# One DMA queue for all maxima, and the queries' staging buffer moved, in the second attention of a one-core kernel

## The reference

```python
B, T, _ = resid.shape                     # 2, 512, 512; 32 heads of 16, 8 key heads, groups of 4
q = (resid @ Wq).reshape(B, T, N_HEADS, D_HEAD).transpose(0, 2, 1, 3)
k = (resid @ Wk).reshape(B, T, N_KV_HEADS, D_HEAD).transpose(0, 2, 1, 3)
v = (resid @ Wv).reshape(B, T, N_KV_HEADS, D_HEAD).transpose(0, 2, 1, 3)
q = q * cos + _rotate_half(q) * sin
k = k * cos + _rotate_half(k) * sin
att = einsum('bhgqd,bhkd->bhgqk', q.reshape(B, 8, 4, T, 16), k) / sqrt(16)
att = where(causal, att, -inf)
ctx = einsum('bhgqk,bhkd->bhgqd', softmax(att), v)
out = ctx.reshape(B, 32, T, 16).transpose(0, 2, 1, 3).reshape(B, T, 512) @ Wo
```

## Time and profile before

| | |
|---|---|
| median of three runs | 950.86 us |
| profiled execution: its own time | 948.68 us |
| profiled execution: span from first to last instruction | 946.9 us |
| PE busy | 912.7 us (96%) |
| DVE busy | 772.8 us (82%) |
| ACT busy | 598.5 us (63%) |
| POOL busy | 617.5 us (65%) |
| attention B from the first exponential | 761.2 us on |
| granted TensorE clock, mean over the span | 0.998 |

### The profile page before, as it was taken

One profiled execution on the slowest core, in us unless ns is written; L12 is line 12 of the kernel. 1 busy time (PEld: TensorE's weight loads), 2 busy tenths in 40 slices (PEclk: granted clock), 3 DMA queues, 4 the chain that ended last, 5 costly groups with the idle time before them and its releaser, 6 DMA issues.

```text
span 946.9 us, 19835 instructions
## 1 busy us (share of the span) xinstructions
PE 912.7 (96%) x6720; PEld 488.5 (52%) x6720; DVE 772.8 (82%) x1812; ACT 598.5 (63%) x1323; POOL 617.5 (65%) x668
## 2 busy tenths in 40 slices
PE   5899999999999999999999999999999989999998
PEld 2455555555555555545555555554545534444553
DVE  6878887887888888687788888888988889996864
ACT  4677666676666666666666666656464469997331
POOL 4788876968768687696877868722459755553211
PEclk9999999999999999999999999999999999999999
DMA  9176386483665637647366564764342943121145
GB/s 338 43 192 173 70 203 136 75 209 87 130 181 107 145 81 192 145 70 205 78 147 176 101 145 96 135 165 86 69 88 53 177 87 58 42 43 24 24 90 156
DMA packets 256005, 114.10 MB, mean 120 GB/s; under 512 B 244144, under 2 KB 244784, under 8 KB 251312
## 3 DMA queue, kind: packets, MB, share of 16 engines
q1 hardware_dynamic: 246400, 70.41, 39.9%
q10 hardware_dynamic: 9520, 42.50, 13.1%
HBM read 49.84 MB, written 2.10 MB: 55 GB/s over the span
## 4 chain that ended last, share of the span: by engine, by line
PE 76%; DVE 11%; ACT 6%; DMA 4%; issue 2%; POOL 1%; SPq 0%; ACTq 0%; DVEq 0%; POOLq 0%
PE bank L1258 15%; PE bank L1259 15%; PE bank L1260 15%; PE bank L1739 4%; PE bank L1357 3%; PE bank L1359 3%; PE bank L1358 3%; PE bank L1377 3%; PE bank L1379 3%; PE bank L1378 3%; PE bank L1671 2%; PE bank L1645 2%; DMA bw_lo<-bw_hi 2%; ACT bank L988 1%; DVE bank L1969 1%
## 5 line engine op out<-in xcount | busy, mean ns | idle before, releaser
L621 POOL TENSOR_TENSOR rt<-rt 128x512 f32<-128x512 f32 x80 | 101.4, 1272 | 133.1 <-DVE rt L1954 133.1
L1986 DVE SCALAR_TENSOR_TENSOR bw_hi<-bank,rden,bw_hi 128x128 f16<-128x128 f32 (+3 forms) x256 | 123.3, 544 | 61.0 <-ACT bw_hi L1024 61.0
L988 ACT ACTIVATE bank<-bank,shift,c_score 128x128 f32<-128x128 f32 (+3 forms) x256 | 147.3, 605 | 2.1
L1969 DVE CUSTOM_DVE_ANT_0 bank<-bank,mask_w 128x512 f32<-128x512 f32 (+3 forms) x256 | 117.9, 521 | 21.5 <-PE bank L1359 21.5
L1024 ACT ACTIVATE bw_hi<-bank,rden 128x128 f16<-128x128 f32 (+3 forms) x256 | 114.5, 535 | 22.7 <-DVE rden L1979 22.7
L983 ACT ACTIVATE shift<-smax,c_score 128x4 f32<-128x4 f32 x64 | 19.0, 297 | 155.5 <-DVE smax L1969 155.5
L628 POOL TENSOR_TENSOR arena<-rt,arena 128x512 f16<-128x512 f32 x80 | 92.3, 1157 | 8.8 <-ACT arena L972 7.9
L1259 PE MATMUL bank<-xt,wq_hi 128*128 128x512 f16 x256 | 97.0, 379 | 0.4 <-issue 0.3
L1258 PE MATMUL bank<-wo_hi,arena 128*128 128x512 f16 x256 | 97.0, 379 | 0.0
L1259 PE MATMUL bank<-wo_lo,arena 128*128 128x512 f16 x256 | 97.0, 379 | 0.0
L1260 PE MATMUL bank<-wo_hi,arena 128*128 128x512 f16 x256 | 97.0, 379 | 0.0
(11 more groups left out here) (241 smaller groups left out, 2455.2 us busy)
## 6 DMA issues: line engine op xcount, KB each, us to landing
qcode<-in_q_codes ACTq DMA_DIRECT2D x7, 1024.0 KB, 4.9
qscale<-in_q_scales ACTq DMA_DIRECT2D x7, 1024.0 KB, 7.2
ocode<-in_o_codes ACTq DMA_DIRECT2D x7, 1024.0 KB, 4.9
oscale<-in_o_scales ACTq DMA_DIRECT2D x7, 1024.0 KB, 7.7
kvcode<-in_k_codes ACTq DMA_DIRECT2D x8, 256.0 KB, 7.5
kvcode<-in_v_codes ACTq DMA_DIRECT2D x8, 256.0 KB, 7.8
kvscale<-in_k_scales ACTq DMA_DIRECT2D x8, 256.0 KB, 8.0
kvscale<-in_v_scales ACTq DMA_DIRECT2D x8, 256.0 KB, 9.6
```

The source lines that it names most:

```text
L988: act.activation(a_rows(i, s), a_rows(i, s), ACT.Exp, bias=shift[:, s % 2, c:c + 1], scale=c_score[:, 0:1], accum_out=bank[3][:, SUMS_AT + ...
L1969: dve.tensor_tensor_reduce(bank[bk][:, o:o + (i + 1) * P], bank[bk][:, o:o + (i + 1) * P], mask_w[:, S - (i + 1) * P:S], 1.0, LOWEST, ALU. ...
L1986: dve.scalar_tensor_tensor(out=p_row[:, s % 2, LO_AT[i]:LO_AT[i] + P_STEP * i + 1:P_STEP], in0=turned_back(i, s), scalar=rden[:, s % 2, c: ...
```

## The change

It has four parts. (1) `q_stack` becomes a view of the second half of `ctx_b`, and with that ScalarE's wait in set 1 goes. (2) ScalarE's two placings are taken off its stream: SyncE issues all of them. (3) `turn_queries` of tiles 6 and 7 leave the place between the first turns of maxima and go to SyncE's rounds 4 and 6; `turn_keys` of tiles 6 and 7, in rounds 3 and 4 before, are in rounds 3 and 5. (4) From set 2 on each placing of pair 0 stands directly behind its own turn, ahead of the turn of pair 1. The separate semaphores of sets 0 and 1 are folded into `d_mturn`.

```diff
-        q_stack = staged("q_stack", [P, 2, B_HEADS * B_ST], F16)
         stage.close()
+        q_stack = ctx_b[:, ST:NT].rearrange("p t n -> p (t n)").bitcast(F16).rearrange("p (i n) -> p i n", i=2)
...
             sp.wait_ge(stacks_set, 2)
             for t in range(NT - 2):
                 turn_queries(t)
                 turn_keys(t)
-            turn_max(0, 0)
-            place_max(sp, 0, 0)
-            turn_max(0, 1)
-            turn_queries(NT - 2)
+            for c in range(2):
+                turn_max(0, c)
+                place_max(0, c)
             turn_max(1, 0)
-            place_max(sp, 1, 0)
             turn_max(1, 1)
-            turn_queries(NT - 1)
+            place_max(1, 0)
+            place_max(1, 1)
             for q in range(2, SETS):
                 turn_max(q, 0)
-                if 3 <= q < 5:
-                    turn_keys(NT - 5 + q)
+                place_max(q, 0)
                 turn_max(q, 1)
-                place_max(sp, q, 0)
-                place_max(sp, q, 1)
+                if q in (3, 5):
+                    turn_keys(NT - 2 + (q - 3) // 2)
+                elif q in (4, 6):
+                    turn_queries(NT - 2 + (q - 4) // 2)
+                place_max(q, 1)
...
-                    if q == 1 and i == 5:
-                        act.wait_ge(d_q[0], 16 * HALF)
-                        act.wait_ge(d_q[1], 16 * HALF)
...
-                if q == 0:
-                    b_exps(q, range(2))
-                    place_max(act, q, 1)
-                    b_exps(q, range(2, LOADS - 2))
-                elif q < SETS:
+                if q < SETS:
                     b_exps(q, range(LOADS - 2))
                 if 1 <= q <= SETS:
                     b_ctx_out(q - 1)
                 if q < SETS:
                     b_exps(q, range(LOADS - 2, LOADS))
-                if q == 0:
-                    place_max(act, 1, 1)
```

More of the change, by code:

```diff
@@ L363, in build @@
         rk1, rk2 = (hs[:, 1, c0:c0 + 2 * P].rearrange("p (i n) -> p i n", i=2) for c0 in (0, 2 * P))
-        staged("before_q_stack", [P, 2, KV_HEADS * 2 * B_ST], F16)
-        q_stack = staged("q_stack", [P, 2, B_HEADS * B_ST], F16)
         stage.close()
+        q_stack = ctx_b[:, ST:NT].rearrange("p t n -> p (t n)").bitcast(F16).rearrange("p (i n) -> p i n", i=2)
         pt = sb("pt", [P, 8, TRI], F32)
@@ L428, in build @@
         d_mturn = [sem(f"d_mturn{c}") for c in range(2)]
-        d_mfirst = [[sem(f"d_mfirst{c}{i}") for i in range(2)] for c in range(2)]
         d_m = [sem(f"d_m{i}") for i in range(3)]
@@ L460, in m_place @@
             return n % 3, 16 * (n // 3 + 1)
[L462 to L473, removed]
         def rows_landed(c, t):
@@ L543, in turn_max, with place_max @@
                 sp.dma_start_transpose(m_turned[:, q % 2, c].rearrange("p (i n) -> p i n", n=P),
-                                       m_stack[:, q % 2, c].rearrange("p i n -> p (i n)")).then_inc(max_turned(q, c)[0], 16)
+                                       m_stack[:, q % 2, c].rearrange("p i n -> p (i n)")).then_inc(d_mturn[c], 16)
+            def place_max(q, c):
+                j, b = set_place(q)
+                sp.wait_ge(d_mturn[c], 16 * (q + 1))
+                for f in range(2):
+                    two = slice(f * P // 2 + MAX_AT, f * P // 2 + MAX_AT + 2)
+                    sp.dma_start(qt_b[two, 2 * j + c, b * S:(b + 1) * S], m_turned[two, q % 2, c]
+                                 ).then_inc(d_mrows[c][q % 2], 16)
             sp.wait_ge(stacks_set, 2)
@@ L802, in _ @@
             twice = float(np.full(2, MAX_W, np.float16).view(np.float32)[0])
-            pool.memset(q_stack[:].rearrange("p i n -> p (i n)").bitcast(F32).rearrange(
+            pool.memset(q_stack.rearrange("p i n -> p (i n)").bitcast(F32).rearrange(
                 "p (g w) -> p g w", w=B_ST // 2)[:, :, MAX_AT // 2:], 0.0).then_inc(stacks_set, 1)
@@ L839, in b_split @@
                 if q >= 2:
-                    pool.wait_ge(*max_turned(q - 2, c))
+                    pool.wait_ge(d_mturn[c], 16 * (q - 1))
                 pool.tensor_tensor(low, m, max_dn[:].unsqueeze(1).broadcast_to([P, ST, 2]), ALU.mult).then_inc(bsplit, 1)
```

## The result

The changed kernel took 964.84 us (median of four runs, 963.87 to 968.37), the kernel before 950.75 on the same terms. The ratio is 1.0161 with a 95% interval of 1.0147 to 1.0176: 15.3 us slower by the ratio (14.1 us lie between the two medians). The profiled execution took 965.24 us at a span of 963.5; before it was 948.68 at 946.9, so 16.6 us lie between the two traces.

| stretch | before | after | difference |
|---|---|---|---|
| span's start to the first exponential | 761.15 | 761.87 | +0.7 |
| to the start of set 2 | 18.22 | 15.75 | -2.5 |
| set 2 to the start of set 6 | 27.06 | 38.06 | +11.0 |
| set 6 to the start of set 15 | 62.84 | 70.50 | +7.7 |
| set 15 and the blocks behind it | 77.6 | 77.3 | -0.3 |

A forecast was written before the change was run, and what follows sets the result against it. PE, ACT and DVE nearly fill attention B's steady part; after the change SyncE's rounds would bind. 5.3 us at set 8, entry gain included, plus 6.0 behind it gave +11.3: 962 on the median, range 954 to 969.

The forecast's parts named there:

- Bound by SyncE's rounds: From set 2 on, two uncovered landings make SyncE's round 7.88 us against 6.76 per set; 6.0 us late by set 14.
- L = 2.65: Landing time of a turn, mean of 27 turns in us; undisturbed 2.3; a half round is L + 1.29.
- The late tile 7: Queries' tile 7 lands at 811.0, holding the first scores of set 8 on PE: 5.3 us later than before.
- The entry's gain: Start of attention B: SyncE placing at once removes PE's 2.6 us wait; gain 3.1 us, between 2.5 and 3.9.
- The 0.6 us of ACT before set 1: Part of the entry's gain: ACT's 1.29 us hole before set 1 shrinks by 0.6 without the DMA issue.
- my sentence against the Trainium skill's rule: At the entry, the trace's 4.22 us to landing disagrees with queues taking turns; by the rule only about 0.9 us won.
- A: Rival: SyncE keeps up in its rounds, only set 8's scores wait; +3.2 to +5.3, 954 to 956 us; chance 0.12.
- B: Rival: faster, the entry's gain stays and nothing is paid in the rounds; 947.8 us; chance 0.07.
- C: Rival: no change, the entry's gain of 3.1 to 3.9 us and the wait at set 8 cancel; chance 0.05.
- D: Rival: clock falls too during PE's stand before set 8; 1 to 3 us more, 963 to 966 us; chance 0.06.
- the last sign: Sign 5: PE's granted clock stays 1.00, as after the earlier 2.58 us stand.
- The wait before 767: Sign 1, at the entry: PE's 2.58 us wait gone, and set 1's exponentials from about 769.5.

The follow-up runs named there:

- the one moved line: From the kernel before, from set 2 on pair 0's placing put ahead of pair 1's turn, nothing else changed: 1.0195, about 18.5 us slower.
- two repaired ones: Changed kernel with both turns ahead of both placings from set 2 (1.0008); the same with tiles between the turns in rounds 2 to 5 (1.0010).
- the kernel with ScalarE's placings and no tile: Kernel with turns first and tiles in rounds 2 to 5, but ScalarE again issues pair 1's placings of sets 0 and 1: 1.0012, 950.95 us.
- keeping the clock up: Changed kernel plus 28 filler matmuls on TensorE ahead of its wait for the tiles of set 8: 1.0170 against the kernel before.
- both turns first: Changed kernel, but from set 2 SyncE issues both turns ahead of both placings, tiles left in rounds 3 to 6: 1.0008, 949.51 us.
- tiles of queries early on SyncE: Kernel before with SyncE issuing all placings, queries' tiles kept between first turns: 1.0038, 953.7 us; with moved stack and no ScalarE wait: 1.0060, 954.88 us.

## Why the prediction was right

**Bound by SyncE's rounds: right, by the mechanism named.** The taken value was 7.88 us per round, from L = 2.65. Measured: the mean landing from set 2 on is 2.64, and the rounds from 7 to 15 took 8.1, or 7.9 without the one wait for a split. That this mean came out so near is partly luck, since it hangs on which turns land late: eight of 28 took over 2.9 us before and seven of 28 after, but only one of them is the same. The seven rounds behind set 8 were to be 6.0 late; sets 6 to 14 lost 7.7. The experiments with the one moved line, put in and taken out, show that this order alone makes the loss.

**The late tile 7: right, roughly a quarter of the loss.** It was to hold PE to 811.0; it did to 814.50, of which 0.7 is the later start of this execution. Of the 2.8 us that are left, 1.3 come from the first start of a turn, (2, 0): 768.6 in the sum, 770.64 in the trace, less the 0.7. The other 1.5 come from the nine halves behind it, which took 38.0 against 36.5; the turn (2, 1) alone landed after 4.2 us instead of 2.65. SyncE in the entry of the changed kernel:

```profile
763.59 3.69 SPq L529 DMA_TRANSPOSE rows<-m_stack  x2
768.13 2.40 SPq L538 DMA_DIRECT2D qt_b<-rows  x4
770.64 1.20 SPq L529 DMA_TRANSPOSE rows<-m_stack  x1
```

The sum lets SyncE's clock start from the split (1, 1) alone, 764.88 and 2.34 us of landing, and gives the turn (1, 0) ahead of it no time of its own. But (1, 0) took 4.5 us to land, so that both placings of set 1 could start only at 768.13. The trace of before had the row: there it took 4.7 (issued 762.56, its placing at 767.29). Three terms of the sum were too small: with the 1.3 it would have been +12.6 and with the 1.5 as well +14.1. Behind set 8 the sum lacks another 1.8 (7.8 us in the traces against 6.0), and 0.7 is the later start; that makes the 16.6 between the traces.

**The entry's gain: size about right, cause half wrong.** Predicted 3.1, measured 2.5 in the changed kernel and 2.8 to 2.9 in two repaired ones. These sizes are differences of single profiles: with the entry as before it took 18.22 us in the kernel before, 18.94 with the stack alone and 20.21 in the kernel with the one moved line, the longer two with the clock down. It is PE's wait that went. The 0.6 us of ACT before set 1 did not come: its hole there is 1.64 us instead of 1.29, since PE waits 0.71 for a placing of set 1. I had the gain from the tile in flight, but the kernel with ScalarE's placings and no tile keeps 2.08 of the 2.58. SyncE's placing leaves ahead of the turn (1, 0), at 762.36 against 763.59, and PE does not wait for it; that this order is what helps fits the profiles and was not tried apart.

With that my sentence against the Trainium skill's rule on turns between queue rows ("DMA: Bandwidth & Descriptors", section on queues, rings and completion order) loses its ground. The 4.22 us were hardly the tile, and the placing's eight packets had moved by 765 while the tile was in flight until 766.9 (760.57 and 6.3 us, the longest of the earlier trace rows). No run here shows that ScalarE's packets waited behind SyncE's.

**The stack costs nothing and brings nothing: right** (0.9998, 0.9989 to 1.0007).

**Rivals.** A fell: the rounds did not stay under 6.76. B and C fell. D held in its first half: the clock fell to 1.2 GHz in PE's stand of 4.56 us ahead of set 8, and once more (0.50 in 849.8 to 853.0) after a stand of 2.06. The Trainium skill says that waits for DMA between bursts of matmuls can bring the clock down ("TensorE: Matmul & The Clock Gate", section on oscillation in real kernels), and the trace agrees. The 2.58 us that had left it at 1.00 before were no safe ground for the last sign: with nearly the same stand at the same step, 2.61 and 2.62 us, the clock fell to 0.50 in the kernel with the stack alone and in the one with the one moved line. D's price of 2 to 3 us fell; keeping the clock up brought no time that the runs can tell.

**Signs.** The wait before 767 went, and set 1 began at 770.97 instead of 769.5. PE waited for placings from set 2 on, not only from set 4. The long wait was there, 4.56 us to 814.50. SyncE's rounds were as said, but it had caught up for sets 7 and 8: ACT has 19.30 us in 820 to 840 and 15.90 in 840 to 860. The clock at 1.00 was wrong (0.83 and 0.91 in two stretches).

**Left open.** No version here is faster than the kernel before; the best, both turns first, is level with it (1.0008, 0.9996 to 1.0020). Whether the entry's 2.8 us can be kept, with tiles 6 and 7 somewhere that costs less, was not found. Nor is it known what makes the turn (1, 0) and ScalarE's placing land late.

## What to carry to other kernels

Before moving work onto a queue that only issues DMAs, add up one round of it with every landing it waits out, and compare with the round of the engines it serves. Take the mean landing and not the undisturbed one: 7.2 us a round against 6.75 would have cost 3 us over seven rounds, 7.9 against 6.75 costs 8, and the traces have 7.8 behind the scores of set 8. A transfer's landing costs its queue little when another issue stands between it and the step that needs it. The same instructions as turn, turn, place, place or as turn, place, turn, place differ by about 18.5 us here, and SyncE's waits for landings by 8.2 against 39.5. And when a transfer is slow in a trace, look at the same transfer in the next variant before naming its neighbour as the cause.

## What the runs showed of the hardware

**Late landings.** The landing of the turn (1, 0) took 4.1 to 4.8 us in ten of the twelve profiles other than that of before (4.7 there), whatever stood beside it, where undisturbed turns take 2.3. In the other two, both with tiles of queries early on SyncE, it took 3.1 and 2.8. In the stretch 763.6 to 768.2 of the changed kernel there are two packets of instructions:

```profile
q8 instruction: 1, 0.02, 2.1%
q14 instruction: 1, 0.01, 1.3%
```

In the profiles of before and after, all 18 turns of attention B that took over 2.9 us had such a packet moving between their issue and their landing. None of the 32 turns without one took that long, and fourteen with one did not either. That speaks for the packets as the cause; no experiment moved them. With the order of before from set 2 on, late landings also recur at a turn: (11, 1) took 3.8 to 4.2 us in all nine such profiles, and at most 3.0 in the four with turn and placing in alternation. So they can be planned for, turn by turn, as long as the order stays.

**The clock.** A stand of about 2.6 us of PE at one and the same step left the granted clock at 1.00 in one profile and brought it to 0.50 in two. In the entry, where the chain of waits goes through PE, the time moves with it: it took 18.22 us with the clock up, 18.94 with 3.4 us at 0.50 and 20.21 with 6.8 us at 0.50. Where SyncE had the last word, 1.00 instead of 0.50 over 6.7 us changed no time that the runs can tell.
